# Another order of the last pieces on VectorE, ScalarE and GpSimd in an adaptive-norm block with a ternary feed-forward

## Time and profile before

| | us |
|---|---|
| median of 3 runs | 338.66 (338.55 to 338.77) |
| the profiled execution's own time | 338.6 |
| its span, first to last instruction | 336.8 |
| busy: TensorE / VectorE / ScalarE / GpSimd | 329.8 / 213.8 / 182.8 / 122.0 |
| granted TensorE clock | 1.000 |

### The profile page before, as it was taken

One profiled execution on the slowest core, in us unless ns is written; L12 is line 12 of the kernel. 1 busy time (PEld: TensorE's weight loads), 2 busy tenths in 40 slices (PEclk: granted clock), 3 DMA queues, 4 the chain that ended last, 5 costly groups with the idle time before them and its releaser, 6 DMA issues.

```text
span 336.8 us, 9812 instructions
## 1 busy us (share of the span) xinstructions
PE 329.8 (98%) x4195; PEld 298.8 (89%) x4195; DVE 213.8 (63%) x418; ACT 182.8 (54%) x354; POOL 122.0 (36%) x111
## 2 busy tenths in 40 slices
PE   8999999999999999999999999999999999999986
PEld 8889989899998989899898999889998889998765
DVE  3656966815859953505167236679565789886896
ACT  2754654454426365356423816478535576638794
POOL 2373505000934762555311413032620123304591
PEclk9999999999999999999999999999999999999999
DMA  7984930500055541210010000100020200200011
GB/s 231 374 291 167 304 129 2 159 1 2 2 147 168 159 157 34 64 33 2 2 55 12 3 20 13 47 19 3 2 62 2 64 3 2 64 1 2 0 33 62
DMA packets 20834, 24.41 MB, mean 72 GB/s; under 512 B 1780, under 2 KB 18328, under 8 KB 20792
## 3 DMA queue, kind: packets, MB, share of 16 engines
q1 hardware_dynamic: 20416, 23.50, 21.9%
q10 hardware_dynamic: 376, 0.30, 0.3%
HBM read 22.68 MB, written 1.11 MB: 71 GB/s over the span
## 4 chain that ended last, share of the span: by engine, by line
PE 93%; ACT 4%; DVE 2%; issue 1%; POOL 0%; ACTq 0%; DVEq 0%
PE proj_banks L564 40%; PE out_bank L564 16%; PE att_banks L657 8%; PE wide_banks L564 5%; PE turn_bank L564 3%; PE proj_banks L627 3%; PE wide_banks L848 3%; PE att_banks L892 2%; PE att_banks L564 2%; PE wide_banks L657 1%; ACT work L1858 1%; PE att_banks L848 1%; PE wide_banks L731 1%; PE proj_banks L848 1%; ACT L1717 1%
## 5 line engine op out<-in xcount | busy, mean ns | idle before, releaser
L1724 ACT ACTIVATE q_t<-proj_banks,bias_cols 128x256 f32<-128x256 f32 x64 | 30.5, 477 | 54.1 <-PE proj_banks L564 54.1
L564 PE MATMUL proj_banks<-x_hi,w_hi 128*128 128x256 f32 x252 | 52.8, 291 | 0.0
L564 PE MATMUL proj_banks<-x_lo,w_hi 128*128 128x256 f32 x252 | 50.7, 283 | 0.0
L564 PE MATMUL proj_banks<-x_hi,w_lo 128*128 128x256 f32 x252 | 50.7, 283 | 0.0
L1231 DVE TENSOR_TENSOR v_sb<-proj_banks,bv_row 128x512 f32<-128x512 f32 x32 | 21.8, 685 | 31.8 <-PE wide_banks L657 30.4
L564 PEld LDWEIGHTS proj_banks<-x_hi,w_hi 128*128 128x128 f32 x252 | 39.5, 191 | 1.5 <-issue 0.4
L564 PEld LDWEIGHTS proj_banks<-x_hi,w_lo 128*128 128x128 f32 x252 | 39.2, 191 | 0.0
L564 PEld LDWEIGHTS proj_banks<-x_lo,w_hi 128*128 128x128 f32 x252 | 39.1, 191 | 0.0
L657 PEld LDWEIGHTS att_banks<-probs_t,v_sb 32*128 32x128 f32 x512 | 29.8, 186 | 5.5 <-issue 5.4
L657 PE MATMUL att_banks<-probs_t,v_sb 32*128 32x32 f32 x512 | 31.6, 272 | 0.0
L1724 ACT ACTIVATE k_t<-proj_banks,bias_cols 128x256 f32<-128x256 f32 x64 | 30.2, 471 | 0.0
(11 more groups left out here) (324 smaller groups left out, 773.9 us busy)
## 6 DMA issues: line engine op xcount, KB each, us to landing
stage<-in_L_cond_qkv_w SPq DMA_DIRECT2D x16, 256.0 KB, 4.5
gate<-gate_rows_scratch SPq DMA_DIRECT2D x48, 64.0 KB, 2.5
stage<-in_L_cond_qkv_w SPq DMA_DIRECT2D x4, 512.0 KB, 5.4
stage<-in_L_cond_out_w SPq DMA_DIRECT2D x4, 512.0 KB, 4.5
work<-in_L_ffn_w SPq DMA_DIRECT2D x2, 1024.0 KB, 9.9
xin<-in_x SPq DMA_DIRECT2D x7, 256.0 KB, 2.9
bv_row<-in_L_cond_qkv_b SPq DMA_DIRECT2D x4, 256.0 KB, 5.4
work<-in_L_cond_ada_w SPq DMA_DIRECT2D x1, 1024.0 KB, 9.3
```

Source lines behind the costliest of these rows:

```text
L564: mm = pe.matmul(dst, l, r, start=start and i == 0, stop=stop and i == len(seq) - 1)
L1724: act.activation(dst[:, h, :], proj_bank[h % 2][:, s * QT:(s + 1) * QT], ACT.Identity, bias=bias_cols[:, c:c + 1]).then_inc(qk_kept, 1)
```

## The change

Four calls move on VectorE, three on ScalarE, two on GpSimd, and one wait of GpSimd's gets a smaller number. No operation is added or taken away.

```diff
@@ VectorE
             last_scale(b, inverse)
+            product = last_product(b)
             last_round(b)
-            product = last_product(b)
             last_deq(b, product)
...
             inverse0 = inverse_of(a, 0, maximum0)
-            scale_of(a, 0, inverse0)
             end_hidden(4, h_tiles)
             end_hidden(5, h_tiles)
+            scale_of(a, 0, inverse0)
+            end_hidden(6, h_tiles)
             dve.wait_ge(h_weighted, 4)
             maximum1 = hidden_max(a, 1, late_hw[1])
-            end_hidden(6, h_tiles)
+            inverse1 = inverse_of(a, 1, maximum1)
             end_hidden(7, h_tiles)
-            inverse1 = inverse_of(a, 1, maximum1)
-            scale_of(a, 1, inverse1)
             dve.wait_ge(h_ready, 4 * b + 4)
             weighed = weigh(h_tiles[1][:, half[1]], g3_row[:, half[1]], late_weighted[:, 1, half[1]])
             dve.wait_ge(h_weighted, 6)
             last_maximum0 = hidden_max(b, 0, late_weighted[:, 0, :])
+            scale_of(a, 1, inverse1)
             last_inverse0 = inverse_of(b, 0, last_maximum0)
             scale_last(0, last_inverse0)
-            round_last(0)
             dve.wait_ge(h_weighted, 7)
             ffn_after(weighed)
             last_maximum1 = hidden_max(b, 1, late_weighted[:, 1, :])
+            round_last(0)
             last_inverse1 = inverse_of(b, 1, last_maximum1)
             scale_last(1, last_inverse1)
             round_last(1)
@@ ScalarE
             load_table(ACT.Silu)
+            end_silu(0)
             keep_q(a, 1, wide_bank[1])
-            end_silu(0)
             end_silu(1)
             square_hidden(a, 0, late_h, 6)
             end_silu(2)
             square(b, 0, late_xa, 5)
+            end_silu(3)
             square(b, 1, late_xa, 5)
-            end_silu(3)
...
             square_hidden(b, 0, None, 8)
+            square_hidden(b, 1, None, 8)
             late_round(0)
-            square_hidden(b, 1, None, 8)
             late_round(1)
@@ GpSimd
-            pool.wait_ge(h_lo_dve, 6)
+            pool.wait_ge(h_lo_dve, 4)
             gate_bias(b, gate1, late_gb)
             ffn_bias(b, late_xa, late_gb)
             pool.wait_ge(g_scaled, 2)
             end_weigh(0, late_hw[0], late_h[0])
-            end_weigh(1, late_hw[0], late_h[0])
             rms_of_both(b)
             hidden_rms(a, 0)
+            end_weigh(1, late_hw[0], late_h[0])
             pool.wait_ge(deq_made, 2 * NQ)
...
             end_weigh(4, late_weighted[:, 0], h_tiles[0])
+            end_weigh(5, late_weighted[:, 0], h_tiles[0])
             hidden_rms(a, 1)
-            end_weigh(5, late_weighted[:, 0], h_tiles[0])
             hidden_rms(b, 0)
             end_weigh(6, late_weighted[:, 1], h_tiles[1])
             hidden_rms(b, 1)
```

## The result

338.98 us (median of 20, 338.80 to 340.96) against 338.71 for the kernel before (20, 338.33 to 339.06): ratio 1.0024, 95% interval 1.0014 to 1.0035. The median is the 339.0 of the prediction, but not all of its terms were there. The 20 executions fall into two groups: 12 from 338.80 to 339.16 (median 338.87), their mean granted clock 0.999 or 1.000, and 8 from 340.09 to 340.96, at 0.994 or 0.995, all above the range's end of 339.8. A median of such a mixture hides the second group as long as it is the smaller.

The account below looks back on a forecast made before the run. TensorE bounds most of the kernel (98% busy), but near the end ScalarE alone is the chain from 322.67 to 329.40. 338.6 + 0.06 + 0.32 = 338.98, say 339.0 us; range 338.5 to 339.8.

Parts of the forecast that it names:

- the term that was to make the loss: ScalarE's last square waits for VectorE's eighth hidden piece near 325.4, moving everything behind it: +0.32 us.
- Step 1: GpSimd's bias operations released at the fourth low half, delaying VectorE's rounding near 306: +0.06 us, bounds 0 and +1.2.
- Steps 2 to 5: First and fourth SiLU, small product and GpSimd's second weighing reordered: zero each, bounds at most +0.2 us.
- Step 6: VectorE's seventh hidden piece ahead of the second maximum, eighth behind: eighth done at 325.36 us instead of 325.00.
- Step 7: ScalarE's last square ahead of the first rounding, waiting for VectorE's eighth piece: +0.32 us, bounds 0 and +0.45.
- Steps 8 and 9: GpSimd's sixth weighing ahead of a root, VectorE's last maximum ahead of a rounding: zero, alone 0.3 us, bound +0.9.
- Step 9: VectorE's last maximum ahead of the other tile's rounding: zero, hidden; 0.3 us if both tail edits stood alone.
- Rival A: Nothing moves, eighth piece in time and the tail's waits hide: 338.5 to 338.8 us, chance 0.24.
- B: GpSimd's last weighing, delayed by blocked roots, sets the end: 339.75 us, chance 0.14.
- C: VectorE's rounding near 306 waits for both bias operations, TensorE's turn 1.2 late: 339.8 to 340.2 us, no separate chance.
- Rival D: TensorE idles from about 325.5 to 327.8, its clock falls to 1.2 GHz for closing work: 341 to 343 us, chance 0.03.

## Why the prediction was right, and where it was not

The median was right (338.98 for 339.0), its sign and size too, and the term that was to make the loss is there in size. Luck had a part: 8 of the 20 executions lie above the whole range, and the median stays near the forecast only because the short ones are the larger group.

- Step 1 (bias operations, +0.06): the mechanism as told, the rounding pair 1.65 us instead of 0.61, the turn unmoved to 0.01 us. The term measured 0, since the rounding ended at 307.40 + 0.20 = 307.60, in time for the turn of 307.68; the bound of 1.2 was far too wide.
- Steps 2 to 5: 0.04 us, told zero with bounds that hold it. GpSimd's root is ready at 316.74 + 0.20 = 316.94, told 316.95, and the scale still starts at 317.03, but lasts 0.03 longer, and what follows it is 0.04 late.
- Step 6: the eighth piece at 324.47, told 324.61 less the trace's lead of 0.16. Right in time, wrong as the main cause: of ScalarE's hole it makes at most 0.06.
- Step 7 (+0.32): right in size, wrong in its main cause. The square starts 0.33 late and the last layer 0.34. With ScalarE's edit alone, where VectorE's piece is early, the square is still 0.27 late (325.25 - 321.50 = 3.75 us instead of 3.48): that is ScalarE's wait for the accumulator read of the square ahead, the `hsq_ready` of `square_hidden`, which the step did not name. VectorE's piece adds 0.06. In the times of the short executions the edit alone costs 0.17 (338.77 in the middle against 338.60), the whole change 0.2 to 0.3 (338.87 against 338.56 to 338.71); these medians of the kernel before take in its upper cluster.
- Steps 8 and 9: hidden behind step 7, as told. The last weighing ends at 328.47, told 328.8 less 0.16. Step 9 alone costs 0.12 us in its trace, not the 0.3 told for both (median +0.09, ratio 1.0003 with an interval across 1).
- Rival A (nothing moves) and B (GpSimd's weighing sets the end) did not happen; nor did C.
- Rival D, the clock, is the larger thing that step 7's edit does. Its mechanism was written down, idle time from 325.5 to 327.8 (measured 325.14 to 327.63) and a half clock after it. Its chance of 0.03 was far too low: it came in 8 executions of 20. Its price, 341 to 343, was too high: the grant stays low for some 3.3 us and not for the whole 4.6 of closing work, and the long executions lie 1.2 to 2.1 above the middle of the short ones. I had read the trace before as safe because the clock was 1.00 at 3.19 busy us of 5. The kernel without four fillers shows how near to the edge that was.

The error that mattered: the prediction sought one time for all executions, and the change made a mixture of two. With the chance at 0.4 it would have given two times and a much larger chance of slower.

What stays open: which property of the stretch decides. Idle ahead of the first turn was 2.49 us (8 of 20 long, and 4 of 12 with GpSimd's wait back at six), 2.19 (6 of 12), 2.09 (5 of 12, VectorE's order undone), 1.16 with 0.51 ahead of the second (4 of 12), 0.87 with 1.52 (8 of 12), and, with none long, 0.87 with 0.57, 1.11 with 0.72 (ScalarE's order undone), 0.77 with 0.57 (both undone) and 0.49 with nothing ahead of the second. No single number of these orders the cases, and their sum does not either: 1.67 has long executions, 1.83 has none. Why one execution falls and the next of the same kernel does not is open too.

## What to carry to other kernels

Filler products and the work between them are one arrangement: where a call moved on another engine makes TensorE's next work late, the fillers must be looked at again, and moved or added with it. Look at all executions and their clocks, not at the median. And before two accumulating operations of one engine are put side by side, look whether the second waits for the first; an operation between them hides that wait.

## What the runs showed of the hardware that was not expected

- In six kernels the clock fell in a third to two thirds of the executions; the shortest idle times among them were 1.16 and 0.51 us, with a turn of 16-bit tiles between. It came back after about 3.3 us in which TensorE had no idle time (329.0 to 332.3 in the changed kernel).
- Two squares with accumulators in a row left 0.17 us between the end of the first one's read and the start of the second when the second waited for the first (128x1024), and 0.08 in another place (128x256).
- The first 22 us differ from execution to execution: TensorE's first scores stood at 20.27 to 20.29 in nine of the 14 traces, and at 20.40, 20.57, 20.64, 21.65 and 21.84 in the others, with a full clock. Taken off the profiled times, the late starts lead to the low end of each kernel's executions: 338.91 - 0.36 = 338.55, 341.77 - 1.37 = 340.40, 339.74 - 1.56 = 338.18. That accounts for these executions, and is the likely source of the cluster 0.4 to 1 us above the lowest that every kernel here shows, the one before included; what makes the start late is not known.
